# Last mixer half of a fused two-layer network: one pass of 512 tokens against two passes of 256

## What is computed

```python
xz = hidden @ W_in.T;  x, z = split(xz)                    # mixer, 1024 inner columns
x = x @ conv_w.T;      out = (x * D * silu(z)) @ W_out.T

logits = x @ gate_w.T                                      # experts
w, sel = top_k(softmax(logits), 8);  w = w / sum(w)
pos  = running count of the tokens that chose this expert before this one
slot = pos if pos < 128 else dropped                       # 64 experts, 128 places each
out[e] = (silu(xin[e] @ wg[e]) * (xin[e] @ wu[e])) @ wd[e]
y[tok] += w * out[e, slot]
```

## Time and profile before

| | us |
|---|---|
| three runs: median (lowest to highest) | 1720.03 (1706.4 to 1729.1) |
| the profiled execution, whole time | 1721.55 |
| its span, first to last instruction | 1719.8 |
| busy in the span: PE, DVE, POOL, ACT | 1505.3, 1050.1, 784.5, 587.1 |

### The profile page before, as it was taken

How to read it: one execution, slowest core, us unless ns; L and a number is a source line. 1 busy time by engine, 2 the same in 40 slices (tenths; PEclk the granted TensorE clock), 3 DMA queues, 4 the chain that set the end, 5 groups by cost and what they waited for, 6 DMA issues and landing times. The chain is left out here.

```text
span 1719.8 us, 18840 instructions
## 1 busy us (share of the span) xinstructions
PE 1505.3 (88%) x5792; PEld 1037.8 (60%) x5792; DVE 1050.1 (61%) x1535; ACT 587.1 (34%) x1050; POOL 784.5 (46%) x483
## 2 busy tenths in 40 slices
PE   6999966899948899988999999999984799998992
PEld 2444423577736777766787778888863455555551
DVE  4887688887889887888988854552443122222220
ACT  4444633344534346343333322121210222222220
POOL 3467853343744444644545425763257223222232
PEclk8999988999979999999999999999996899999996
DMA  6899663356654667657565557997760799999986
GB/s 205 253 285 281 195 221 134 98 158 191 201 155 138 214 204 225 206 171 258 166 188 167 176 168 278 377 357 237 249 201 26 222 324 324 321 319 307 307 218 126
DMA packets 193539, 380.39 MB, mean 221 GB/s; under 512 B 20994, under 2 KB 95106, under 8 KB 192944
## 3 DMA queue, kind: packets, MB, share of 16 engines
q1 hardware_dynamic: 165360, 322.89, 59.4%
q0 software_dynamic: 20032, 39.92, 9.7%
q10 hardware_dynamic: 8064, 16.55, 2.8%
HBM read 301.65 MB, written 124.35 MB: 248 GB/s over the span
## 5 line engine op out<-in xcount | busy, mean ns | idle before, releaser
L1518 POOL TENSOR_TENSOR y<-y,hc 128x2048 f32<-128x2048 f32 x64 | 293.1, 4579 | 250.3 <-DVE hc L1350 250.3
L598 PE MATMUL bank<-tokT,ring 128*128 128x512 f32 x768 | 308.7, 402 | 12.4 <-DVE xall L1202 7.1
L1332 DVE TENSOR_TENSOR_SCAN bx<-bank,state,bx 128x512 f32<-128x512 f32 x256 | 312.5, 1265 | 0.8
L600 PE MATMUL bank<-tokT,ring 128*128 128x512 f32 x768 | 303.1, 395 | 0.0
L599 PE MATMUL bank<-tokT,ring 128*128 128x512 f32 x768 | 302.6, 394 | 0.0
L975 ACT ACTIVATE bank<-dl,an 128x512 f32<-128x512 f32 x256 | 171.0, 684 | 332.3 <-DVE bx L1332 332.2
L1524 POOL TENSOR_TENSOR act<-th,act 128x512 fp32r<-128x512 f32 x88 | 116.0, 1318 | 261.0 <-ACT act L899 260.4
L854 PE MATMUL bank<-wgu,xeT 128*128 128x384 f32 x512 | 178.2, 492 | 0.0
L598 PEld LDWEIGHTS bank<-tokT,ring 128*128 128x128 f32 x768 | 146.7, 191 | 48.6 <-issue 17.2
L610 PE MATMUL bank<-ring,act 128*128 128x512 f32 x352 | 145.2, 412 | 24.6 <-DVE th L1182 19.3
L600 PEld LDWEIGHTS bank<-tokT,ring 128*128 128x128 f32 x768 | 146.2, 190 | 32.2
(11 more groups left out here) (151 smaller groups left out, 2010.7 us busy)
## 6 DMA issues: line engine op xcount, KB each, us to landing
ring<-w_all SPq DMA_DIRECT2D x286, 512.0 KB
wgu<-wgu_in SPq DMA_DIRECT2D x64, 768.0 KB
wde<-wd_in SPq DMA_DIRECT2D x64, 384.0 KB
slots<-empty_in SPq DMA_DIRECT2D x16, 1154.0 KB, 8.4
w_all<-staged_u SPq DMA_DIRECT2D x64, 256.0 KB, 3.4
xe<-slots ACTq DMA_DIRECT2D x56, 288.5 KB
w_all<-fst SPq DMA_DIRECT2D x48, 256.0 KB, 3.9
w_all<-staged_d SPq DMA_DIRECT2D x32, 256.0 KB, 3.8
```

The source lines that it names most:

```text
L598: nc.tensor.matmul(b[:, :], w[:, k, 0, :], x[:, 0, k, :], start=(k == 0), stop=False)
L600: last = nc.tensor.matmul(b[:, :], w[:, k, 1, :], x[:, 0, k, :], start=False, stop=(k == KT - 1))
L1332: nc.vector.tensor_tensor_scan(bx[:, k, :], dA[k % 2][:, :], bx[:, k, :], state[:, k, n:n + 1], ALU.mult, ALU.add).then_inc(S_sc, 1)
L1518: nc.gpsimd.tensor_tensor(y[c % 2][:, :, :], y[c % 2][:, :, :], hc[:, :, :], ALU.add).then_inc(S_ya, 1)
```

## The change

The last half of the last mixer chunk is now two halves of the same eight pairs, the first for tokens 0 to 255 of the chunk (tiles 12 and 13), the second for tokens 256 to 511 (tiles 14 and 15). Gate and up quanta of both have 256 columns where they had 512, in twelve matmuls as before; so have tanh, the copies and the three elementwise operations. The first pass has its own eight down quanta, of six matmuls of 512 columns each, in the loop; the second pass has `tail(2)` and `tail(3)`. Every gate and up block of weights is loaded twice, and the eight down blocks too. Tiles 8 to 13 are routed in the loop, one every 6 positions, and only 14 and 15 behind it. The second pass takes the banks in the other order (`pair_banks`), because the first pass's sums stand in `PF[0]` and `PF[1]`.

```diff
-MIX = [[("mixer", c, part, 4 * part, 4) for part in range(2)] for c in range(NCH - 1)] + [[("mixer", NCH - 1, 0, 0, M1)]]
+MIX = [[("mixer", c, part, 4 * part, 4) for part in range(2)] for c in range(NCH - 1)] + [[("mixer", NCH - 1, part, 0, M1) for part in range(2)]]
...
+LASTS = (len(HALVES) - 2, len(HALVES) - 1)
+ADDS = TT * (len(HALVES) - 1)
+
+
+def columns(h):
+
+    return slice(CH // 2 * LASTS.index(h), CH // 2 * LASTS.index(h) + CH // 2) if h in LASTS else slice(0, CH)
+
+
+def tiles_of(h):
+    return range(2 * LASTS.index(h), 2 * LASTS.index(h) + 2) if h in LASTS else range(TT)
+
+
+def pair_banks(h, j):
+
+    first = 2 * ((j + (h == LASTS[1])) % 2)
+    return first, first + 1
...
-            TAIL = TURN + 12 + 2 * M1
+            HALF1 = TURN + 12 + 3 * M1
+            TAIL = HALF1 + 2 * M1
             spread([("mixer", 2, 0), ("ffn", 3, 0), ("ffn", 3, 1)], range(START, TURN))
-            spread([("mixer", 2, 1), ("mixer", 3, 0)], range(TURN, TAIL + RING))
+            spread([("mixer", 2, 1), ("mixer", 3, 0), ("mixer", 3, 1)], range(TURN, TAIL + RING))
...
-            route_at = [DRAIN + 12 + 5 * i for i in range(EARLY)] + [TURN + 12 + 4 * i for i in range(TT)]
+            route_at = [DRAIN + 12 + 5 * i for i in range(EARLY)] + [TURN + 12 + 6 * i for i in range(TT)] + [HALF1, HALF1 + 6]
...
-                        if pos == TAIL - 6:
+                        if pos == TURN + 26:
                             sp.wait_ge(n4.xn, 2 * TT + 2)
                             sp.wait_ge(S_x3, 16 * 3)
                             load_weights(5, 5)
-                        if pos == TAIL - 1:
+                        if pos == HALF1 + 2:
                             sp.wait_ge(n4.xn, 3 * TT)
                             load_weights(6, 6)
-                        if pos == TAIL + 2:
+                        if pos == TAIL:
+                            sp.wait_ge(S_up, sum(pairs_of))
                             load_weights(7, 7)
...
+                                elif h == LASTS[1]:
+                                    pe.wait_ge(*((S_gt, i) if j == 0 else (S_de, adds_to(h) + 2)))
...
-                                nc.tensor.matmul(b[:, :], w[:, k, 0, :], x[:, 0, k, :], start=(k == 0), stop=False)
...
+                                nc.tensor.matmul(b[:, cols], w[:, k, 0, :], x[:, 0, k, cols], start=(k == 0), stop=False)
...
-                        for t in range(TT):
+                        for t in tiles_of(h):
...
-                            if (t, j) == (0, 0):
-                                pe.wait_ge(S_de, TT * h)
+                            if (t, j) == (2, 0):
+                                pe.wait_ge(S_gt, first_pair[h] + M1 - 1)
...
-                    place(11)
-                    tail(0, range(M1))
-                    tail(1, first_part)
-                    route_T(12)
-                    tail(1, second_part)
-                    logits(12)
-                    tail(2, first_part)
-                    place(12)
-                    route_T(13)
-                    tail(2, second_part)
-                    logits(13)
+                    tail(2, range(M1))
                     tail(3, first_part)
-                    place(13)
                     route_T(14)
                     tail(3, second_part)
                     logits(14)
+                    place(14)
                     route_T(15)
-                    place(14)
                     logits(15)
                     place(15)
...
-                            if h == len(HALVES) - 1 and kind == "up":
+                            if h in LASTS and kind == "up":
                                 gated_lo(h, j)
...
                     side(TAIL + 1)
-                    rows_out(10, 6)
-                    rows_out(10, 7)
-                    for k in range(3):
-                        rows_out(11, k)
-                    rstd(12)
-                    for k in range(3, TOPK):
-                        rows_out(11, k)
-                    rstd(13)
-                    rows_out(12, 0)
-                    rows_out(12, 1)
                     rstd(14)
-                    for k in range(2, TOPK):
-                        rows_out(12, k)
                     rstd(15)
-                    for i in range(13, 16):
+                    for i in (14, 15):
                         for k in range(TOPK):
                             rows_out(i, k)
```

More of the change, by code:

```diff
@@ L341, in before_half @@
                     return None
-                return half_of[kind, c, part - 1] if part else half_of["ffn", c, 1]
+                return half_of[kind, c, part - 1] if part and h not in LASTS else half_of["ffn", c, 1]
             with nc.Block() as block:
@@ L582, in quantum @@
                             x = tokT[c % 2]
-                            b = PF[2 * (j % 2) + (0 if kind == "gate" else 1)]
+                            cols = columns(h)
+                            b = PF[pair_banks(h, j)[0 if kind == "gate" else 1]]
                             if kind == "gate":
@@ L893, in tanh @@
                         wait(act, S_al, i - 1)
-                        nc.scalar.activation(th[:, i % 2, :], PF[2 * (j % 2)][:, :], ACT.Tanh, scale=gsh[:, m:m + 1]).then_inc(S_th, 1)
+                        cols = columns(h)
+                        nc.scalar.activation(th[:, i % 2, cols], PF[pair_banks(h, j)[0]][:, cols], ACT.Tanh, scale=gsh[:, m:m + 1]).then_inc(S_th, 1)
                     def gated_hi(h, j):
@@ L898, in gated_hi @@
                         i = first_pair[h] + j
-                        nc.scalar.activation(act8[:, 0, j, :], th[:, i % 2, :], ACT.Copy).then_inc(S_ah, 1)
+                        cols = columns(h)
+                        nc.scalar.activation(act8[:, 0, j, cols], th[:, i % 2, cols], ACT.Copy).then_inc(S_ah, 1)
                     def prep_hi(i, m):
@@ L1108, in _ @@
                     side(TAIL + 1)
-                    for i in range(3 * TT, NCH * TT):
+                    for i in range(len(route_at), NCH * TT):
                         route_T(i)
@@ L1173, in half_gated @@
                         dve.wait_ge(S_th, i + 1)
[L1175 removed]
+                        cols = columns(h)
+                        nc.vector.scalar_tensor_tensor(out=th[:, i % 2, cols], in0=th[:, i % 2, cols], scalar=1.0, in1=PF[pair_banks(h, j)[0]][:, cols],
                                                        op0=ALU.add, op1=ALU.mult).then_inc(S_hg, 1)
@@ L1190, in gated_lo @@
                         dve.wait_ge(S_ah, i + 1)
-                        nc.vector.tensor_tensor(act8[:, 1, j, :], th[:, i % 2, :], act8[:, 0, j, :].bitcast(fp32),
+                        cols = columns(h)
+                        nc.vector.tensor_tensor(act8[:, 1, j, cols], th[:, i % 2, cols], act8[:, 0, j, cols].bitcast(fp32),
                                                 ALU.subtract).then_inc(S_al, 1)
@@ L1528, in side @@
                         for h, kind, j in quanta_at.get(pos - 2, ()):
-                            if kind == "up" and h < len(HALVES) - 1:
+                            if kind == "up" and h not in LASTS:
                                 gated_lo(h, j)
```

33 lines of the change are left out of this document (13 added, 20 removed).

## The result

| | before | after |
|---|---|---|
| four runs each: median (lowest to highest), us | 1723.36 (1706.4 to 1729.1) | 1744.49 (1738.66 to 1745.69) |
| profiled execution, span, us | 1721.55, 1719.8 | 1745.69, 1743.9 |
| `rstd(8)` to the end of the last `rows_out`, us | 117.1 | 135.8 |

The ratio of the times is 1.011, with a 95% interval of 1.0071 to 1.0149. Timed once more later, with both kernels on one chip, it is 1.0102 (1.006 to 1.0144), medians 1732.2 and 1716.1. The change makes the kernel slower by 16 to 21 us.

What follows compares the result with a forecast made beforehand. POOL's last `rows_out` was taken to bound the experts' start. Eight fewer at the end save 10.2 us, loops and second pass cost 22: +12.2 on 1721.55 gives 1733.7, taken as 1733 us; range 1710 to 1750.

Steps and rivals of the forecast that it cites:

- The loop of one tile: Tiles 8 to 13, `rstd` to next `rstd` through four `rows_out`: 13.8 us, up to 15.2 where PE's clock falls.
- The work per quantum: PE's 256-column gate and up matmuls: 0.120 us each, so a half-width quantum takes 1.44 us (1.37 to 2.3).
- DVE's and ACT's half-width operations: Half-width operations behind each quantum: 0.40 us each, between 0.34 and 0.75.
- From the second pass to tile 14: From `rstd(13)` at 1295.1 through the last quanta and `tail(2)` to tile 14's first `rows_out` at 1330.4.
- Sixteen `rows_out`: POOL's rows of tiles 14 and 15 at the very end: 20.2 us.
- The end: POOL's last `rows_out` in the changed kernel ends at 1350.6.
- The step that failed: POOL's end in the changed kernel, 1350.6, set against 1338.4 in the profile before: +12.2 us.
- in the drain one tile takes 14.5 us: Kernel before, a tile of chunk 2 in the drain: 14.5 us from `rstd` to `rstd`, read from its profile.
- Rival 1: Faster: POOL's four `rows_out` are not in the loop and PE sets the pace; 1707 us, chance 0.16.
- rival 2: Slower: each half-width matmul waits for its weight load, a quantum takes 2.3 us; 1744 us, chance 0.12.
- Rival 3: Slower: PE's signals come some 2 us late on `logits` in the last four loops; 1742 us, chance 0.20.
- DMA at 0: 24 more ring loads, 12.6 MB, priced at 0 us, range 0 to +3, hidden by POOL's slowness.

Runs made afterwards that it cites:

- e5_rstd_first_pause: Changed kernel with `rstd` ahead of all eight `rows_out` and two tiny POOL instructions between the fourth and fifth; ratio to before 1.0048.
- e2_before_four_ahead: Kernel before with only POOL's order changed: four `rows_out` of tiles 8 to 11 ahead of the next `rstd`; ratio to before 1.0061.
- e4_pause: Changed kernel with two tiny POOL instructions between the fourth and fifth `rows_out` of tiles 8 to 13; ratio to before 1.0123.
- e9_after_again: Changed kernel, no edit, profiled a second time; 129.3 us from `rstd(8)` to the last `rows_out`, ratio to before 1.0102.
- e12_loads_late_alone: Changed kernel with only the loads of experts 4, 5 and 6 moved behind the last gate/up quantum; ratio to before 1.0106.
- e10_tail_order: `e6_loads_late` with tile 14's logits, routing and first `rows_out` put ahead of tile 15's steps in the tail; ratio to before 0.9999.
- e6_loads_late: `e5_rstd_first_pause` with the loads of experts 4, 5 and 6 moved behind the last gate/up quantum; ratio to before 1.0034.
- e8_before_pause: Kernel before with two tiny POOL instructions between the fourth and fifth `rows_out` of tiles 8 and on; ratio to before 1.0033.
- e1_rstd_first: Changed kernel with POOL's order undone, `rstd` ahead of all eight `rows_out` from tile 8 on; ratio to before 1.0066.
- e7_before_again: Kernel before, no edit, profiled a second time; 109.8 us from `rstd(8)` to the last `rows_out`.

## Why the prediction was right, and where its size came from

- *The loop of one tile* held. Forecast 13.8, 15.2, 15.2, 14.4, 15.2; the first profile has 13.61, 15.67, 15.62, 13.69, 14.73, the second 13.63, 15.70, 15.11, 16.09, 14.90: in sum 73.8 against 73.3 and 75.4. `e5_rstd_first_pause` and `e2_before_four_ahead` show that POOL's order makes it: 12.7 us of the changed kernel's stretch go with it (against `e4_pause`), and 8.6 to 15.9 come with it in the kernel before.
- *The work per quantum*, 0.120 us a matmul, measured 0.12. Here the Trainium skill's page "TensorE: Matmul & The Clock Gate", section "Back-to-back issue gap", bears: 109 ns by its formula for one matmul of 256 columns. By it, as an estimate, a quantum would be 0.13 us shorter than measured, and 40 of them 5 us. DVE's and ACT's half-width operations, priced at 0.40, took 0.42 to 0.48; from the quantum's end to `MAX8` it took 1.22 to 1.64 in `e9_after_again`, priced at 1.4.
- *From the second pass to tile 14*: `rstd(13)` to tile 14's first `rows_out` was forecast at 35.3 us. It is 33.7 undisturbed and 42.2 in the first profile, where held signals put the ring's last two loads 5.2 us late. *Sixteen `rows_out`*, 20.2 us, are 20.2 (1340.91 to 1361.12).
- *The end*: forecast 129.3 us from `rstd(8)` (1350.6 - 1221.3); `e9_after_again` has 129.3. So the absolute sum for the changed kernel was right for an undisturbed execution, but in part by luck: the five loops took 1.6 us more than forecast (one of them, tile 11 to 12, 16.1 instead of 14.4), and the piece behind them 1.6 us less, since of the 1.3 us added there for the ring only 0.4 came. Tile 11 to 12 took 13.7 in the first profile and in `e12_loads_late_alone`; why it is either, no run shows.
- **The step that failed** is the other side of the subtraction: "POOL ends at 1350.6, against 1338.4". The 1338.4 was read from one execution of the kernel before, that held signals had made 7.3 us longer; undisturbed the last `rows_out` ends 109.8 behind `rstd(8)`, not 117.1. I set a clean sum against a disturbed profile, and +12.2 should have been +19.5. The timed medians put the whole change at 16 to 21 us. The same error stands in "in the drain one tile takes 14.5 us": undisturbed it takes 12.9 ((1260.08 - 1221.44) / 3).
- *Rival 1* (PE sets the pace) and *rival 2* (weight loads) fell: intervals of 14 to 16 us, and 0.12 us a matmul. `e10_tail_order` reaches 10.5 to 12.7 us a tile once the order is undone, and even then is only level with before.
- *Rival 3* (late signals) named a real mechanism, and its 1742 lies nearest to the first median, 1744.5. But it put the delay on `logits` of the last four loops, and held that before partly hid it. In the first profile it sat behind tile 13's rows, at the ring's last loads, and in before it cost as much. In the second pair of profiles it did not appear, and the ratio was the same, so it is not what makes the changed kernel slower.
- *DMA at 0*: right only because POOL was slower, as written ("were that gone, the ring would be next"): gone, the ring cost 7.0 us (`e5_rstd_first_pause` against `e6_loads_late`).

Where the expected gain went: eight `rows_out` fewer stood at the end and saved 10.2 us, but the new positions put half of each tile's rows ahead of the next tile's `rstd`. With order and ring mended and the pause in both, two passes and one pass have the same stretch, 112.8 (`e6_loads_late`) and 112.9 us (`e8_before_pause`), and ratios of 1.0034 and 1.0033. These two, `e4_pause` and `e5_rstd_first_pause` were timed together and are all undisturbed: of the 19.6 us between the two kernels with the pause (132.5 and 112.9), 12.7 are POOL's order and 7.0 the ring.

## What to carry to other kernels

Before subtracting a forecast from a profile, see whether that profile holds waits without a releaser ("remote"), and take a second one; if it does, a sum of clean steps must be set against a clean base, or the waits be added to both. When work is spaced differently by position numbers, write out each in-order queue at the new spacing: which step of the older tile now stands ahead of the first step of the next. Then ask what is next behind the bound: here the order was worth 12.7 us and, once it was mended, the ring 7.0, while mending the ring alone showed nothing (`e12_loads_late_alone`). And before crediting a cure, see that the profile without it and the one with it are alike where the cure does not reach: here they were not.

## What the hardware showed that was not expected

- In four profiles signals of PE were held back while POOL issued `rows_out` without a break, up to 6.0 us, from some 5 us into a run of eight until at most 2 us behind its end. In the first profile of before three of them then came within 0.16 us (1262.03 to 1262.19), so the work had been done and only its signals were held. As far as their records are kept, signals of ACT, DVE and POOL showed nothing of it. The Trainium skill's page "Perfetto Trace Analysis", section "Tensor Engine Instruction (MATMUL, LD_WEIGHTS)", says that a matmul's end in the profile is an estimate and that its semaphore is pushed when PSUM has acknowledged the write. The trace agrees that the two can lie apart, by 6.0 us at most; where all records are kept they lie 0.02 us apart or less.
- They do not always come, and it is not the chip: on one chip `e1_rstd_first` had ten and, later, `e5_rstd_first_pause` had none, even in the unbroken runs of eight ahead of tile 8. They came only in profiles that had lost semaphore records. Whether the recording of the profile, the many `rows_out` or a third thing holds them stays open. It was not tried.
- A pause of 0.73 us between eight `rows_out` cost 3.1 us of stretch in both kernels where no signal was held (`e8_before_pause` against `e7_before_again`, `e4_pause` against `e9_after_again`, one profile of each, on two chips). That it helps where signals are held is not shown.
